# Eight products that nobody reads, and a subtraction one place earlier, in the prologue of a fused RWKV and gated-MLP kernel

## The chip, the cores and the metric

The kernel runs on one core of a Trainium2 chip. The metric is the device time of one execution in microseconds (us); for a kernel it is the median over its runs. The engines are called as in the profile: PE (TensorE, matrix products; PEld is its weight load), DVE (VectorE), ACT (ScalarE), POOL (GpSimd) and SP (SyncE, which here issues every DMA).

## The reference, cut to what matters

For `x` of 4 x 2048 x 512 float32, the layer adds two branches to its input. Both start from the normalised rows:

```python
def _layernorm(x, axis=-1, eps=1e-05):
    m = jnp.mean(x, axis=axis, keepdims=True)
    v = jnp.var(x, axis=axis, keepdims=True)
    return (x - m) / jnp.sqrt(v + eps)

xn = _layernorm(x, axis=-1)
# attention branch: shifted = xn one token later
xk = mu_k * xn + (1.0 - mu_k) * shifted      # the same for xr, xv
k = jnp.einsum('btc,hc->bth', xk, Wk)        # the same for r, v
wkv = wkv_v4(k, v, wkv_w, wkv_u)             # a recurrence over the tokens
attn = jnp.einsum('bth,ch->btc', jax.nn.sigmoid(r) * wkv, Wo)
# MLP branch
hidden = jax.nn.silu(xn @ W1.T) * (xn @ W3.T)
mlp = fwht(hidden) @ W2.T                    # Walsh-Hadamard transform
out = x + attn + mlp
```

The kernel applies the Walsh-Hadamard transform once, to `W2`, in its prologue.

## The kernel before, in words

The 8192 tokens are worked off in 8 pairs of two blocks of 512 tokens. For each pair there are 16 steps with the up weights (`up_step`), then 24 units with the weights of k, v and r of the next pair (`r_unit`) in turn with 20 down products. Every number is split into a rounded high part and a low rest, so each product of a 128 x 128 weight tile takes three matmuls, L953 to L955 in `r_unit`: twelve matmuls for a unit. ACT makes the high part, DVE (inputs, L1403) or POOL (weights, L751, first pair alone) the low part. The weights are split during the first pair and stored; from the second pair on they are only loaded.

Every engine has its own program, in the order in which it is written; semaphores join them. The change lies in the prologue, ahead of pair 0:

- The inputs of the first pair lie in `xt`, channels on partitions. To normalise them, the mean and the reciprocal deviation of each token must stand in every partition. DVE takes the statistics of the rows (`token_stats`, `token_mean_var`, `add_eps`). `make_diagonal(0, 0)` (L1354) puts the 4 x 128 means on diagonals of 128 x 128 tiles, and `spread_tokens(0)` on PE (L977) multiplies them by a matrix of ones, `had[:, 3, :]`; four products fill bank `acc[0]` with the mean of every token. The same is done with the reciprocal deviation, which POOL makes (L745), by `make_diagonal(0, 1)`, into `acc[1]`.
- `centre(0, 0, pair)` (L1368) subtracts `acc[0]` from two of the four channel tiles of the first 512 tokens, `scale(0, 0, pair)` (L1380) multiplies them by `acc[1]`. `centre` waits for the first half of `xt` and for the four products of the means; `scale` for the four products of the deviations.
- Then the inputs of unit n are mixed: ACT `mix_first` (L1035), DVE `mix_item` (L1394), ACT `mix_second` (the high part, L1047), DVE `mix_rest` (the low part, L1403), and PE multiplies. There are three buffers: `mix_second(n)` waits from n = 3 on for unit n - 3 to be done.
- After units 0 to 8 PE makes the first half of the transform of `W2` (`turn_within_tiles`, L988: sixteen products of a constant float32 matrix by a float32 tile of 512 columns), spreads the tokens of the second block (L977 again), and goes on with the units. After unit 14 comes the second half (L967), then the rest and pair 0.
- DVE computes the statistics of the second block, `first_stats(1)` (L1322 and behind), between the mixing for units 4 and 5.

Of the kernel before, what the change touches and what calls it, by code (L numbers as in the profile page):

```python
# [128 lines left out]
def build(nc, x, x_t, w_units, vectors, hadamard, out):  # L129
# [15 lines left out]
    with ctx:  # L145
        def sb(name, shape, dt=f32, stack=ctx):
            return stack.enter_context(nc.sbuf_tensor(name, shape, dt))
# [6 lines left out]
        acc = [ctx.enter_context(nc.psum_tensor(f"acc{i}", [P, C], f32)) for i in range(TT)]  # L154
# [23 lines left out]
        with ExitStack() as early:  # L178
            had = sb("had", [P, 4, P], f32, early)
# [108 lines left out]
        def wait(eng, s, t, k):  # L288

            value = t * per[s.name] + k  # L290
            if not isinstance(value, int) or value > 0:
                eng.wait_ge(s, value)
# [504 lines left out]
        def _(pe):  # L797
# [136 lines left out]
            def r_unit(r, n):  # L934

                g, kt = divmod(n, KT)
                w = r_weights(r, n)
                m_in = mix[n % MIX_AHEAD]
                wait(pe, mix_hi, r, n + 1)
                wait(pe, mix_lo, r, n + 1)  # L940
                for m in range(KT):
                    if kt == 0 and g:
                        wait(pe, kvr_ready, r, KT * (g - 1) + m + 1)
                    elif kt == 0:
                        if m == 0:
                            wait(pe, ha_full, r - 1, FT)
                        elif m == 1:
                            wait(pe, gate_a_sum, r - 1, FT)
                        else:
                            wait(pe, gate_b_sum, r - 1, FT)  # L950
                    col = slice(m * P, (m + 1) * P)
                    bank = r_bank[m]
                    pe.matmul(bank[:, :], w[:, 0, col], m_in[:, 0, :], start=kt == 0, stop=False)  # L953
                    pe.matmul(bank[:, :], w[:, 1, col], m_in[:, 0, :], start=False, stop=False)  # L954
                    last = pe.matmul(bank[:, :], w[:, 0, col], m_in[:, 1, :], start=False, stop=kt == KT - 1)  # L955
                    if m == KT - 1:
                        last.then_inc(r_done, 1)
                    elif kt == KT - 1:
                        last.then_inc(r_bank_done, 1)

            def turn_across_tiles():

                wait(pe, xt_ready, 0, 4)
                for n, j in enumerate(TILES_TURNED):
                    pe.wait_ge(turned_loaded[j * W2_LOADS // FT], 16)
                    pe.wait_ge(w2_copied, FT + n + 1 - TT)
                    pe.matmul(acc[j % TT][:, :], had[:, 1, :], fly[0][:, j, :], start=True, stop=True)\  # L967
                        .then_inc(w2_psum, 1)

            def spread_tokens(h):  # L970

                for a in range(2):
                    if h:
                        pe.wait_ge(w2_copied, FT - 1 + a)
                    for t in range(TT):
                        pe.wait_ge(diagonal_made, 2 * TT * h + TT * a + t + 1)
                        last = pe.matmul(acc[2 * h + a][:, t * P:(t + 1) * P], had[:, 3, :], diagonal[:, a, t, :],  # L977
                                         start=True, stop=True)
                    last.then_inc(spread, 1)

            def turn_within_tiles():

                wait(pe, xt_ready, 0, 2)
                for j in range(FT):
                    pe.wait_ge(w2_loaded[j * W2_LOADS // FT], 16)
                    if j >= TT:
                        pe.wait_ge(w2_copied, j + 1 - TT)
                    pe.matmul(acc[j % TT][:, :], had[:, 0, :], fly[0][:, j, :], start=True, stop=True)\  # L988
                        .then_inc(w2_psum, 1)

            pe.wait_ge(had_loaded, 16)
            spread_tokens(0)
            for n in range(R_UNITS):
                r_unit(0, n)
                if n == PASS_ONE_AFTER:
                    turn_within_tiles()
                    spread_tokens(1)
                if n == PASS_TWO_AFTER:
                    turn_across_tiles()
# [310 lines left out]
        def _(dve):  # L1310
            def wide(a):
                return a.broadcast_to([P, 2, N])
# [29 lines left out]
            def columns(h, pair):  # L1342
                return xt[:, 2 * pair:2 * pair + 2, 1 + h * N:1 + (h + 1) * N]

            def spread_row(h, a):
                return acc[2 * h + a][:, :].rearrange("p (o n) -> p o n", o=1)

            def make_diagonal(h, a):

                if h:  # L1350
                    dve.wait_ge(spread, a + 1)
                    dve.wait_ge(rstd_ready if a else mean_copied, 2)
                for t in range(TT):
                    dve.tensor_scalar(diagonal[:, a, t, :], had[:, 2, :], mean_rstd[:, h, a, t:t + 1], None, ALU.mult)\  # L1354
                        .then_inc(diagonal_made, 1)

            def centre(r, h, pair):

                first = isinstance(r, int) and r == 0
                if pair == 0:  # L1360
                    if first:
                        dve.wait_ge(xt0_loaded[h], 16)
                        dve.wait_ge(spread, 2 * h + 1)
                    else:
                        wait(dve, xt_loaded, r - 1, 64)
                        wait(dve, tok_loaded, r - 1, 16 * (h + 1))
                a = columns(h, pair)
                dve.tensor_tensor(a, a, wide(spread_row(h, 0) if first else tok[:, 0:1, :]), ALU.subtract)\  # L1368
                    .then_inc(centred, 1)

            def scale(r, h, pair):

                first = isinstance(r, int) and r == 0
                wait(dve, centred, r, 2 * h + pair + 1)
                if first:
                    dve.wait_ge(spread, 2 * h + 2)
                elif h == 0 and pair == 1:
                    wait(dve, tok_stored, r - 1, 32)
                a = columns(h, pair)
                dve.tensor_tensor(a, a, wide(spread_row(h, 1) if first else tok[:, 1:2, :]), ALU.mult)\  # L1380
                    .then_inc(xt_ready, 1)
# [336 lines left out]
                .then_inc(const_made, 1)  # L1718
            dve.wait_ge(decay_made, 2)
            dve.wait_ge(pro_step, 8)  # L1720
            dve.wait_ge(rstd_ready, 1)
            make_diagonal(0, 1)
            centre(0, 0, 0)
            scale(0, 0, 0)
            centre(0, 0, 1)
            mix_item(0, 0)
# [71 lines left out]
```

## Time and profile before

| | us |
|---|---|
| median of 3 runs | 2708.76 (2707.26 to 2709.22) |
| the profiled execution | 2706.29 |
| its span, first to last instruction | 2704.5 |
| PE busy | 2658.3 (98%) |
| DVE busy | 2177.0 (80%) |
| ACT busy | 1328.5 (49%) |
| POOL busy | 237.0 (9%) |

Busy times of PE overlap in their ends, since a matmul is started before the one ahead of it has left the array: the start of one matmul to the start of the next is the better measure, and a row with the first and last start of a group gives it. PEclk is the granted clock of PE as a share of 2.4 GHz.

### The profile page before, as it was taken

How to read it: one execution, taken by the hardware profiler on the slowest of the kernel's cores; microseconds unless marked ns; L12 is line 12 of the kernel's file. 1: busy time of each engine (PE TensorE's matmuls, PEld its weight loads, DVE VectorE, ACT ScalarE, POOL GpSimd, SP SyncE). 2: the span in 40 equal slices, each digit the busy share in tenths (PEclk: the TensorE clock that was granted, in tenths of full speed). 3: DMA queues.
4: the chain of work that ended last, by engine and by line, in shares of the span. 5: the costliest groups of instructions: out<-in, count | busy, mean ns of one | idle time of the engine just before them, and what ended most of it. 6: DMA issues, size and time to landing. Idle time of an engine off the chain costs nothing.

```text
span 2704.5 us, 33906 instructions
## 1 busy us (share of the span) xinstructions
PE 2658.3 (98%) x11616; PEld 2178.5 (81%) x11616; DVE 2177.0 (80%) x2938; ACT 1328.5 (49%) x2117; POOL 237.0 (9%) x180
## 2 busy tenths in 40 slices
PE   7999999999999999999999999999999999999998
PEld 5677787888888888888888888888888888888887
DVE  7888888888868888688887888868888788878784
ACT  6765564444554446444464445544455444544442
POOL 3388800000000000000000000000000000000000
PEclk9999999999999999999999999999999999999999
DMA  7787786877868778687787867778687777866677
GB/s 274 293 300 256 280 287 221 278 241 244 286 218 280 241 249 279 231 271 235 254 277 240 279 217 270 259 247 271 216 278 248 261 258 232 273 240 221 230 227 267
DMA packets 244952, 691.51 MB, mean 256 GB/s; under 512 B 31920, under 2 KB 31920, under 8 KB 244272
## 3 DMA queue, kind: packets, MB, share of 16 engines
q1 hardware_dynamic: 244784, 689.34, 75.7%
q8 instruction: 97, 1.59, 0.2%
q14 instruction: 71, 0.58, 0.1%
HBM read 575.94 MB, written 113.30 MB: 255 GB/s over the span
## 4 chain that ended last, share of the span: by engine, by line
PE 89%; DVE 5%; POOL 2%; ACT 1%; issue 1%; DMA 1%; SPq 0%; ACTq 0%; DVEq 0%
PE gamma L871 12%; PE gamma L874 12%; PE gamma L873 12%; PE acc L881 10%; PE acc L883 10%; PE acc L882 10%; PE gamma L953 4%; PE gamma L955 4%; PE gamma L954 4%; PE alpha L871 2%; PE alpha L873 2%; PE alpha L874 2%; PE alpha L955 1%; PE alpha L953 1%; PE alpha L954 1%
## 5 line engine op out<-in xcount | busy, mean ns | idle before, releaser
L1069 ACT ACTIVATE step<-gamma 128x512 f32<-128x512 f32 x512 | 306.3, 598 | 823.1 <-PE gamma L874 807.1
L871 PE MATMUL gamma<-xs_high,wring 128*128 128x512 f32 x1280 | 499.3, 390 | 12.2 <-DVE step L1522 5.4
L873 PE MATMUL gamma<-xs_high,wring 128*128 128x512 f32 x1280 | 498.4, 389 | 0.0
L874 PE MATMUL gamma<-xs_low,wring 128*128 128x512 f32 x1280 | 498.4, 389 | 0.0
L881 PE MATMUL acc<-vring,hid 128*128 128x512 f32 x1232 | 481.0, 390 | 8.2 <-POOL vring L751 4.0
L883 PE MATMUL acc<-vring,hid 128*128 128x512 f32 x1232 | 479.6, 389 | 0.0
L882 PE MATMUL acc<-vring,hid 128*128 128x512 f32 x1232 | 479.6, 389 | 0.0
L871 PEld LDWEIGHTS gamma<-xs_high,wring 128*128 128x128 f32 x1280 | 240.5, 188 | 65.5 <-issue 8.6
L881 PEld LDWEIGHTS acc<-vring,hid 128*128 128x128 f32 x1232 | 231.4, 188 | 62.4 <-issue 9.1
L874 PEld LDWEIGHTS gamma<-xs_low,wring 128*128 128x128 f32 x1280 | 240.5, 188 | 50.2
L873 PEld LDWEIGHTS gamma<-xs_high,wring 128*128 128x128 f32 x1280 | 240.5, 188 | 49.6
L883 PEld LDWEIGHTS acc<-vring,hid 128*128 128x128 f32 x1232 | 231.4, 188 | 48.1
L882 PEld LDWEIGHTS acc<-vring,hid 128*128 128x128 f32 x1232 | 231.5, 188 | 47.4
L1394 DVE SCALAR_TENSOR_TENSOR step<-xt,vec,step 128x512 f32<-128x512 f32 x192 | 144.8, 758 | 141.9 <-ACT step L1035 141.3
L1047 ACT ACTIVATE mix<-step 128x512 fp32r<-128x512 f32 x192 | 120.8, 629 | 239.7 <-PE gamma L955 187.4
L1482 DVE RECIPROCAL z<-z 128x512 f32<-128x512 f32 x64 | 214.1, 3345 | 0.0
L953 PE MATMUL gamma<-mix,wring 128*128 128x512 f32 x522 | 203.6, 390 | 4.6 <-ACT kvr L1062 2.6
L955 PE MATMUL gamma<-mix,wring 128*128 128x512 f32 x522 | 203.1, 389 | 0.0
L954 PE MATMUL gamma<-mix,wring 128*128 128x512 f32 x522 | 203.1, 389 | 0.0
L745 POOL TENSOR_TENSOR mean_rstd<-var_eps,half 128x4 f32<-128x4 f32 x16 | 23.1, 1447 | 1882.7 <-DVE var_eps L1340 1882.7
L1530 DVE TENSOR_TENSOR step<-step,alpha 128x512 f32<-128x512 f32 x128 | 86.4, 675 | 120.9 <-PE alpha L874 101.7
L1403 DVE TENSOR_TENSOR mix<-step,mix 128x512 fp32r<-128x512 f32 x192 | 137.7, 717 | 20.7 <-ACT mix L1047 10.3
(177 smaller groups left out, 4745.3 us busy)
## 6 DMA issues: line engine op xcount, KB each, us to landing
wring<-u_split SPq DMA_DIRECT2D x336, 512.0 KB, 4.2
vring<-d_split SPq DMA_DIRECT2D x288, 512.0 KB, 4.3
wring<-r_split SPq DMA_DIRECT2D x168, 512.0 KB, 4.2
raw<-spilled SPq DMA_DIRECT2D x160, 256.0 KB, 4.2
spilled<-step SPq DMA_DIRECT2D x128, 256.0 KB, 4.3
wlast<-u_split SPq DMA_DIRECT2D x112, 256.0 KB, 3.1
u_split<-wring SPq DMA_DIRECT2D x48, 512.0 KB, 3.9
res<-x SPq DMA_DIRECT2D x16, 1024.0 KB, 8.2
```

Of the source, the lines that this page charges most:

```text
L871: pe.matmul(bank[:, :], w[:, 0, col], high, start=fresh and kt == 0, stop=False, skip_group_check=True)
L873: pe.matmul(bank[:, :], w[:, 1, col], high, start=False, stop=False, skip_group_check=True)
L874: last = pe.matmul(bank[:, :], w[:, 0, col], low, start=False, stop=kt == 1, skip_group_check=True)
L881: pe.matmul(acc[tt][:, :], a[:, 0, col], w[:, 0, :], start=first, stop=False)
L882: pe.matmul(acc[tt][:, :], a[:, 1, col], w[:, 0, :], start=False, stop=False)
L883: return pe.matmul(acc[tt][:, :], a[:, 0, col], w[:, 1, :], start=False, stop=final)
L953: pe.matmul(bank[:, :], w[:, 0, col], m_in[:, 0, :], start=kt == 0, stop=False)
L954: pe.matmul(bank[:, :], w[:, 1, col], m_in[:, 0, :], start=False, stop=False)
L955: last = pe.matmul(bank[:, :], w[:, 0, col], m_in[:, 1, :], start=False, stop=kt == KT - 1)
L1069: act.activation(to, bank[:, :], ACT.Copy).then_inc(u_copied, 1)
L1394: dve.scalar_tensor_tensor(f, xt[:, kt, 1 + h * N:1 + (h + 1) * N], vec[:, q, kt:kt + 1], f, ALU.mult, ALU.add).then_inc(mix_full, 1)
L1482: dve.reciprocal(z[:, 1, :], z[:, 1, :]).then_inc(wkv_step, 1)
```

## The change

Two edits, both ahead of unit 0. PE issues eight products of the constant matrix of ones by the constant tiles `had` (512 float32 columns) between `spread_tokens(0)` and unit 0; they go to `acc[2]` and `acc[3]` in turn, wait for nothing, signal nothing, and what they leave there is overwritten by the next product that starts in these banks. And DVE subtracts the mean from the first two channel tiles, `centre(0, 0, 0)`, ahead of the second diagonal instead of behind it.

```diff
             pe.wait_ge(had_loaded, 16)
             spread_tokens(0)
+            for i in range(8):
+                pe.matmul(acc[2 + i % 2][:, :], had[:, 3, :], had[:, :, :].rearrange("p a q -> p (a q)"),
+                          start=True, stop=True)
             for n in range(R_UNITS):
                 r_unit(0, n)
...
             dve.wait_ge(decay_made, 2)
             dve.wait_ge(pro_step, 8)
+            centre(0, 0, 0)
             dve.wait_ge(rstd_ready, 1)
             make_diagonal(0, 1)
-            centre(0, 0, 0)
             scale(0, 0, 0)
             centre(0, 0, 1)
```

DVE before, from the diagonals of the means to the mixing for the first two units (`tok` holds the diagonals, `acc` the spread values):

```order
L1354 TENSOR_SCALAR tok<-had,mean_rstd 128x128 x4
L1717 TENSOR_SCALAR one_less_mu<-vec 128x12
L1354 TENSOR_SCALAR tok<-had,mean_rstd 128x128 x4
L1368 TENSOR_TENSOR xt<-xt,acc 128x2x512
L1380 TENSOR_TENSOR xt<-xt,acc 128x2x512
L1368 TENSOR_TENSOR xt<-xt,acc 128x2x512
L1394 SCALAR_TENSOR_TENSOR step<-xt,vec,step 128x512 x2
```

DVE in the changed kernel, the same place (its lines stand three further down the file):

```order
L1357 TENSOR_SCALAR tok<-had,mean_rstd 128x128 x4
L1720 TENSOR_SCALAR one_less_mu<-vec 128x12
L1371 TENSOR_TENSOR xt<-xt,acc 128x2x512
L1357 TENSOR_SCALAR tok<-had,mean_rstd 128x128 x4
L1383 TENSOR_TENSOR xt<-xt,acc 128x2x512
L1371 TENSOR_TENSOR xt<-xt,acc 128x2x512
L1397 SCALAR_TENSOR_TENSOR step<-xt,vec,step 128x512 x2
```

The first subtraction has gone ahead of the four diagonals of the deviation; nothing else moved on DVE.

PE at the start of its program, as a difference (`first_r` holds the split weights of units 0 to 3):

```order
 L796 UNCONDITIONAL_BRANCH
 L977 MATMUL acc<-tok,had 128x128 x8
+L994 MATMUL acc<-had 128x512 x8
 L953 MATMUL gamma<-mix,first_r 128x512
 L954 MATMUL gamma<-mix,first_r 128x512
```

The eight products stand between the products that spread the tokens and the first matmul of unit 0.

## Rows read from the trace of the kernel before

**Rows 1.** The page: busy time of PE, and the chain that ended last by engine.

```profile
PE 2658.3 (98%) x11616; PEld 2178.5 (81%) x11616; DVE 2177.0 (80%) x2938; ACT 1328.5 (49%) x2117; POOL 237.0 (9%) x180
...
PE 89%; DVE 5%; POOL 2%; ACT 1%; issue 1%; DMA 1%; SPq 0%; ACTq 0%; DVEq 0%
```

**Rows 2.** Windows (us): busy us (and count) by engine, clock, DMA share, GB/s.

```profile
0.00:130.00 130.00, 111.91 (x429) 80.06 (x430) 102.89 (x143) 89.88 (x149) 39.03 (x33) 0.99 0.76 281
...
340.00:2704.00 2364.00, 2351.68 (x10349) 1940.57 (x10347) 1895.52 (x2611) 1114.47 (x1760) 18.41 (x13) 1.00 0.76 252
```

**Rows 3.** Timeline of DVE: start us, us, what, [idle before <-releaser].

```profile
7.72 0.87 DVE L1354 TENSOR_SCALAR tok<-had,mean_rstd 128x128 f32<-128x128 f32 x4
...
9.21 0.87 DVE L1354 TENSOR_SCALAR tok<-had,mean_rstd 128x128 f32<-128x128 f32 x4 [0.54 <-POOL mean_rstd L745]
10.31 1.22 DVE L1368 TENSOR_TENSOR xt<-xt,acc 128x1024 f32<-128x1024 f32 x1 [0.22 <-PE acc L977]
12.02 1.22 DVE L1380 TENSOR_TENSOR xt<-xt,acc 128x1024 f32<-128x1024 f32 x1 [0.48 <-PE acc L977]
...
24.21 1.80 DVE L1403 TENSOR_TENSOR mix<-step,mix 128x512 fp32r<-128x512 f32 x1
...
26.60 1.79 DVE L1403 TENSOR_TENSOR mix<-step,mix 128x512 fp32r<-128x512 f32 x1
28.31 1.27 DVE L1322 BATCH_NORM_STATS2 stats<-x 128x6 f32<-128x512 f32 x2
...
31.64 0.75 DVE L1394 SCALAR_TENSOR_TENSOR step<-xt,vec,step 128x512 f32<-128x512 f32 x1
32.30 0.69 DVE L1403 TENSOR_TENSOR mix<-step,mix 128x512 fp32r<-128x512 f32 x1
```

**Rows 4.** Timeline of PE: tokens spread, first matmuls of units 0, 1, 5, and L988.

```profile
8.15 3.75 PE L977 MATMUL acc<-tok,had 128*128 128x128 f32 x16 [8.15 <-DVE tok L1354]
...
16.57 0.76 PE L953 MATMUL gamma<-mix,first_r 128*128 128x512 f32 x1 [4.66 <-DVE mix L1403]
...
20.71 0.40 PE L953 MATMUL gamma<-mix,first_r 128*128 128x512 f32 x1
...
33.13 0.47 PE L953 MATMUL gamma<-mix,wring 128*128 128x512 f32 x1 [1.03 <-ACT mix L1047]
...
44.12 4.45 PE L988 MATMUL acc<-fly,had 128*128 128x512 f32 x10
```

**Rows 5.** Matmuls of three lines (L977 twice): ns min/median/max, first and last start.

```profile
L977 PE MATMUL acc<-tok,had x16: 421/421/552, 8.2 to 11.5; 128*128 128x128 f32 x16
...
L977 PE MATMUL acc<-tok,had x16: 275/275/369, 57.9 to 59.6; 128*128 128x128 f32 x16
...
L988 PE MATMUL acc<-fly,had x32: 590/592/592, 44.1 to 57.4; 128*128 128x512 f32 x32
```

**Rows 6.** Windows of PE alone: busy us (and count), clock, DMA share, GB/s.

```profile
12.58:15.99 3.41, 0.00 (x0) 1.00 1.05 386
15.99:19.40 3.41, 2.83 (x7) 0.50 1.05 387
...
234.44:237.86 3.42, 3.42 (x10) 0.50 0.28 104
```

**Rows 7.** Timeline of PE before and behind the second low-clock stretch.

```profile
233.59 0.47 PE L871 MATMUL gamma<-xs_high,wring 128*128 128x512 f32 x1 [3.30 <-DVE step L1522]
...
249.73 0.47 PE L881 MATMUL acc<-vring,hid 128*128 128x512 f32 x1 [1.34 <-POOL vring L751]
```

**Rows 8.** Timeline of ACT: the high parts for units 3 and 4.

```profile
22.27 0.63 ACT L1047 ACTIVATE mix<-step 128x512 fp32r<-128x512 f32 x1 [0.62 <-DVE step L1394]
...
24.33 0.63 ACT L1047 ACTIVATE mix<-step 128x512 fp32r<-128x512 f32 x1 [0.30 <-DVE step L1394]
```

**Rows 9.** Timeline of POOL: two weight splits.

```profile
24.11 1.36 POOL L751 TENSOR_TENSOR wring<-res,wring 128x512 fp32r<-128x512 f32 x1 [0.71 <-ACT wring L1160]
...
26.18 1.67 POOL L751 TENSOR_TENSOR vring<-res,vring 128x512 fp32r<-128x512 f32 x1 [0.71 <-ACT vring L1160]
```

## The prediction, made before the changed kernel ran

> **What bounds the kernel now.** I read the page first: PE is busy 98% of the span and holds 89% of the chain that ended last [rows 1]. By stage it is the same picture with one weak place: from 340 us on PE is busy 2351.7 of 2364 us, in the first 130 us only 111.9 of 130 [rows 2]. So a stall in the prologue has no slack to vanish into later: whatever PE does later there, the steady part behind it starts later. The change touches only the stretch up to 44 us, so the next view is the timeline there, engine by engine. The reader is to see three things.
>
> First, DVE sets the start. The means' diagonals start at 7.72 and PE answers at 8.15, 0.43 later; the deviation's diagonals run from 9.21 to 10.08; the first subtraction starts at 10.31, released by PE's first four products, and the first scaling at 12.02, released by the next four [rows 3, 4]. Unit 0 starts at 16.57, when its inputs are mixed, after PE sat idle for 4.66 us [rows 4].
>
> Second, the clock. PE runs the sixteen matmuls of the spread from 8.2 to 11.5, a pitch of 3.3 / 15 = 0.22 us; the same sixteen take 57.9 to 59.6 later, 1.7 / 15 = 0.11 us [rows 5]. So the first ones ran at 1.2 GHz, though no low clock is recorded for them. Then the records show the high level from 12.58 to 15.99 with PE idle, the low one from 15.99 to 19.40, and the high one again [rows 6]: the fall follows the idle time, the rise comes 2.8 us after PE restarted at 16.57. Unit 0 therefore takes 20.71 - 16.57 = 4.14 us. Four units at the high clock take 44.12 - 33.13 = 10.99, 2.75 each [rows 4], so the low clock costs unit 0 1.39 us.
>
> Third, unit 5, at 33.13, is where PE last waits in this stretch, 1.03 us [rows 4]. What it waits for is DVE: the statistics of the second block from 28.31, then the mixing for unit 6 at 31.64 and the low part for unit 5 at 32.30, which ends at 32.99 [rows 3]. From 33.13 to 44.12 and into the transform PE has no gap. So the change is worth what it moves unit 5.
>
> **The subtraction moved.** It waits for the first four spread products, and these end where they did: the subtraction had waited 0.22 us for PE behind the second diagonals, not for DVE [rows 3]. It cannot start before 10.31. The slot it leaves, 9.21 to 10.08, was filled with the second diagonals beside PE's work; now DVE waits there, and the diagonals start behind the subtraction, at 10.31 + 1.22 = 11.53. From the start of the first diagonals to the start of what waits for their products took 10.31 - 7.72 = 2.59 us, at the low clock (0.43 to PE, 2.16 from there). So the first scaling starts at 11.53 + 2.59 = 14.12 instead of 12.02: +2.1 us. At the high clock eight matmuls with a pitch of 0.11 instead of 0.22 save 0.8 to 0.9: +1.2. No cover hides it, since all mixing waits for it. Nothing is gained in exchange; a gain would need the subtraction earlier, which the 0.22 us excludes.
>
> **The eight products.** The trace shows their like: L988 is a constant float32 matrix by 512 float32 columns; 32 matmuls for sixteen products from 44.1 to 57.4, a pitch of 13.3 / 31 = 0.43 us at the high clock [rows 5]. Eight products are 16 matmuls: 6.9 us at the high clock, 13.7 at the low one. They start behind the spread: its second half starts at 11.53 + 0.43 = 11.96 and takes 8 x 0.213 = 1.7, so 13.7. The 4.66 us of idle that they are put into is shorter than the cheapest of the two. Where the clock rises at time w, they end at 13.7 + 6.9 + (w - 13.7) / 2. In before the high level stood at the latest 12.58 - 8.15 = 4.4 us after PE first started and came 2.8 us after it restarted; 2.8 to 4.4 behind 11.96 is w = 14.8 to 16.4. I take w = 16, the end of the range, because PE also pauses from about 10.2 to 11.96: end at 21.7. The bounds: high throughout, with a spread that ends at about 13.1, gives 20.0; w = 19.4 gives 23.4; never gives 27.4.
>
> Unit 0's inputs are ready at 16.57 + 2.1 = 18.7, so the products, not the inputs, now hold unit 0. It starts at 21.7 at the high clock: +5.1 on its start, but it takes 2.75, not 4.14, +3.7 on its end. Units 0 to 4 back to back are 5 x 2.75 = 13.7, so PE could start unit 5 at 35.4, +2.3; the rest of the +3.7 goes into the 1.03 us before unit 5 and small gaps before it.
>
> DVE comes out alike. The high part of unit 3 waits for unit 0 to be done: 21.7 + 2.75 + 0.2 = 24.65, against 22.27, +2.4; that of unit 4 for unit 1: 27.4, against 24.33, +3.1 [rows 8]. DVE is busy with earlier low parts in between, so the statistics start +2.4 to +2.8 late, and unit 5 with them. The two do not add: one late start of unit 5, the later of PE's +2.3 and DVE's +2.4 to +2.8. I take +2.6.
>
> The DMA queue is no price: the loads of W2, issued behind splits that shift too, are needed at 44.12 + 2.6.
>
> By the Trainium skill's page "TensorE: Matmul & The Clock Gate" (What's actually happening), the throttled clock is the default and activity releases it, which speaks for the products as warm-up; the low stretch behind the idle time agrees. Its whole worth here would be the 1.39 us of unit 0, and the sum without the products' own length would be 1.39 us shorter, not 2.6 longer.
>
> Two low parts, at 24.21 and 26.60, take 1.8 us where that at 32.30 takes 0.69 [rows 3]; POOL's splits started at 24.11 and 26.18, ahead of them [rows 9]. If shifted starts avoid one, DVE is 1.1 us earlier, but PE's 35.4 then holds unit 5: +2.3 stays. The page "SBUF — State Buffer" of the Trainium skill (SBUF: two separate sides) calls the pair of ports that the two engines share an exclusive lock held for the whole instruction; these rows agree.
>
> **Behind 44 us** all is moved by the same amount. One term can differ: a second low stretch, 234.44 to 237.86, after an idle time of 3.30 us [rows 6, 7]. If it falls away, PE gains up to 3.42 / 2 = 1.7 us; but PE then waits 1.34 us for POOL at 249.73, so most of it would only lengthen that wait. I take 0, with -1.7 to +1.7 as bounds.
>
> **Sum.** The profiled execution: 2706.29 + 2.6 = 2708.9. It lies 2.5 under the median, so the forecast for the median is 2708.76 + 2.6 = 2711.4.
>
> **The rivals.**
> - High clock from the start (17%): the high level of 12.58 is granted here too. For it: the record. Then products end at 20.0, unit 5 by PE at +0.6, DVE at +1.2 to +1.5: about 2710.1.
> - Late rise (17%), w = 19.4, since the pause at 10.2 counts against the rise: products end at 23.4, unit 5 at +4.0: 2712.8.
> - The clock never rises before unit 0 (5%): products end at 27.4, unit 5 at +8.0: 2716.8. Against: in before it rose within 2.8 us of dense work.
> - Absorbed (9%): later waits of pair 0, such as 3.30 and 1.34 us [rows 7], turn out to wait for something that did not shift. Against: DMA and all engines hang on PE's transform. 2708.8.
> - The clock pays, the other side (4%): with the high clock from the start (+1.2) and the second low stretch gone (-1.7), the kernel is faster, 2708.3. Place: 234 us; it decides once the shift is under 1.7 us and pair 0 there waits for PE, against which POOL's wait speaks. A version in which unit 0's 1.39 us also counts would need the products done by 16.6, which the pitch of L988 excludes.
>
> **How the numbers follow.** The forecast, with a shift of 2.3 to 2.8, has 48%: 2711.4. A measurement tells 0.2%, 5.4 us, from no change. Only the never-rising clock passes it, so slower by over 0.2% has 5% and 3 more for spread and for two terms at their far ends together: 8%. Faster by as much follows from no case; 2% for what I don't see. Within 0.2%: 90%. The range goes from 2707.6 (the clock pays, and a run 0.7 low) to 2715.2 (late rise, +1.7 of the second stretch and 0.7).
>
> **What would show it.** In the profile of the changed kernel: DVE idle from about 8.7 to 10.3, the subtraction still at 10.31, the scaling at about 14.1 (13.2 would be the high clock); the new matmuls at a pitch of 0.85 and then 0.43, end near 21.7; unit 0 with a pitch of 0.23 and 2.75 us long; unit 5 near 35.7 and the transform near 46.7; the same shift at the end. Wrong would be a scaling at 12.0, products with a pitch of 0.23 or less, or a transform shifted by over 2 us with an end that is not.

## The result, and the profile after

| | before | changed |
|---|---|---|
| median of 22 runs each, in turn | 2707.97 us (2703.52 to 2712.24) | 2711.95 us (2706.88 to 2715.96) |
| ratio, 95% interval | | 1.0013 (1.0008 to 1.0019) |
| profiled execution, its span | 2706.29, 2704.5 | 2706.88, 2705.1 |

The changed kernel is slower by 0.13%, 3.5 us (2.2 to 5.1 by the interval; the two medians themselves stand 4.0 us apart). The profiled execution of it happens to be the quickest of its 22, only 0.6 us above that of before; why is told below. Where the time goes must be read at the start.

DVE of the changed kernel answers to [rows 3]:

```profile
10.31 1.22 DVE L1371 TENSOR_TENSOR xt<-xt,acc 128x1024 f32<-128x1024 f32 x1 [1.66 <-PE acc L977]
11.45 2.46 DVE L1357 TENSOR_SCALAR tok<-had,mean_rstd 128x128 f32<-128x128 f32 x4
15.34 1.22 DVE L1383 TENSOR_TENSOR xt<-xt,acc 128x1024 f32<-128x1024 f32 x1 [1.42 <-PE acc L977]
...
30.89 1.80 DVE L1406 TENSOR_TENSOR mix<-step,mix 128x512 fp32r<-128x512 f32 x1
32.61 1.27 DVE L1325 BATCH_NORM_STATS2 stats<-x 128x6 f32<-128x512 f32 x2
...
36.59 0.69 DVE L1406 TENSOR_TENSOR mix<-step,mix 128x512 fp32r<-128x512 f32 x1
```

The subtraction starts at 10.31 to the hundredth, as before. The four diagonals behind it take 2.46 us, not 0.87, and the first scaling starts at 15.34, 3.3 us late. Three views show why, in this order: the diagonals singly (ns min/median/max, first and last start), POOL's work beside them, and the timeline of PE, which answers to [rows 4]:

```profile
L1357 DVE TENSOR_SCALAR tok<-had,mean_rstd x4: 273/564/1298, 11.4 to 13.6; 128x128 f32<-128x128 f32 x4
```

```profile
10.95 2.49 POOL L751 TENSOR_TENSOR first_r<-raw,first_r 128x512 fp32r<-128x512 f32 x2 [1.90 <-ACT first_r L1163]
```

```profile
8.13 2.05 PE L977 MATMUL acc<-tok,had 128*128 128x128 f32 x8 [8.13 <-DVE tok L1357]
12.36 0.80 PE L977 MATMUL acc<-tok,had 128*128 128x128 f32 x2 [2.18 <-DVE tok L1357]
13.58 1.65 PE L977 MATMUL acc<-tok,had 128*128 128x128 f32 x6 [0.42 <-DVE tok L1357]
15.02 8.34 PE L994 MATMUL acc<-had 128*128 128x512 f32 x16
22.80 0.80 PE L953 MATMUL gamma<-mix,first_r 128*128 128x512 f32 x1
...
25.96 0.39 PE L953 MATMUL gamma<-mix,first_r 128*128 128x512 f32 x1
...
37.42 0.47 PE L953 MATMUL gamma<-mix,wring 128*128 128x512 f32 x1 [0.39 <-ACT mix L1050]
```

POOL splits the first two weight tiles from 10.95 to 13.44, about 1.25 us each. Taken singly, the first diagonal runs from 11.45 to 12.30 and the second from 12.22 to 13.52; the splits end at 12.22 and 13.44. So each of the two diagonals ends 0.08 us behind the end of a split, and the other two, with POOL idle, take 0.27 us each. The same 0.08 stands in the two other profiles with this order and POOL beside it (the changed kernel again, and the move alone). POOL's own row for these splits in the kernel before, which no diagonal met there, since the last one ended at 10.08:

```profile
10.80 2.49 POOL L751 TENSOR_TENSOR first_r<-raw,first_r 128x512 fp32r<-128x512 f32 x2 [1.73 <-ACT first_r L1160]
```

PE gets the first diagonal's work at 12.36 and the second's at 13.58. The products start at 15.02 and the last begins at 22.8; unit 5 starts at 37.42 instead of 33.13, +4.3, and the transform, by the row below, at 48.45 instead of 44.12. The products have their forecast pitch: the row of L994 (ns min/median/max, first and last start), the windows of PE (busy, clock, DMA share, GB/s), which answer to [rows 5, 6], and PE at the transform:

```profile
L994 PE MATMUL acc<-had x16: 592/592/1061, 15.0 to 22.8; 128*128 128x512 f32 x16
```

```profile
15.02:17.65 2.63, 2.63 (x5) 1.00 1.06 389
17.65:22.80 5.15, 5.15 (x14) 1.00 0.79 267
22.80:25.96 3.16, 3.16 (x15) 1.00 0.79 245
140.53:143.94 3.41, 3.31 (x8) 0.50 0.83 266
234.44:237.86 3.42, 0.12 (x2) 1.00 0.89 326
```

```profile
48.45 1.02 PE L988 MATMUL acc<-fly,had 128*128 128x512 f32 x2
```

Up to 17.65 us four of the new matmuls start (five with the last of the spread), behind that one every 0.43 us: the clock was low until about there, though the column says 1.00, since the records start only at 17.65. Unit 0 runs at the high clock: behind the last product, which ends at about 23.2, it takes 2.75 us. ACT's high part for unit 3 waits for it, at 26.21 instead of the 22.27 of [rows 8]:

```profile
26.21 0.63 ACT L1050 ACTIVATE mix<-step 128x512 fp32r<-128x512 f32 x1 [1.27 <-PE gamma L955]
```

By the windows the stretch of low clock at 234 us [rows 6] is missing in this execution, and one at 140 us is there.

### The profile page after: what moved, and what is told of

Same layout as the page of the kernel before. It is cut to its first block, busy times and chain, and to the rows that moved or that the text cites. A ratio compares the mean times of both kernels' runs of the same rounds, so it can differ in the third digit from the quotient of the medians.

```text
span 2705.1 us, 33938 instructions
## 1 busy us (share of the span) xinstructions
PE 2664.4 (98%) x11632; PEld 2181.5 (81%) x11632; DVE 2176.6 (80%) x2938; ACT 1328.1 (49%) x2117; POOL 236.7 (9%) x180
## 4 chain that ended last, share of the span: by engine, by line
PE 89%; DVE 5%; POOL 3%; ACT 1%; issue 1%; DMA 1%; SPq 0%; ACTq 0%; DVEq 0%
PE gamma L871 12%; PE gamma L874 12%; PE gamma L873 12%; PE acc L881 10%; PE acc L883 10%; PE acc L882 10%; PE gamma L953 4%; PE gamma L955 4%; PE gamma L954 4%; PE alpha L871 2%; PE alpha L874 2%; PE alpha L873 2%; PE alpha L953 1%; PE alpha L955 1%; PE alpha L954 1%
## 5 line engine op out<-in xcount | busy, mean ns | idle before, releaser
L882 PEld LDWEIGHTS acc<-vring,hid 128*128 128x128 f32 x1232 | 231.4, 188 | 47.4
L745 POOL TENSOR_TENSOR mean_rstd<-var_eps,half 128x4 f32<-128x4 f32 x16 | 22.6, 1414 | 1880.2 <-DVE var_eps L1343 1880.2
```

The lines of the kernel that those rows point to most:

```text
L882: pe.matmul(acc[tt][:, :], a[:, 1, col], w[:, 0, :], start=False, stop=False)
```

## The experiments

What a profile's matmuls show is given as the start of the transform (44.12 in the kernel before), since the same matmul can be found in each; beside it stands the start of DVE's first scaling. Except in the last column each figure is of one execution. The ratio compares with the kernel before, run in turn with it.

| | transform at | first scaling at | median, ratio (95%) |
|---|---|---|---|
| before, changed | 44.12, 48.45 | 12.02, 15.34 | 1.0013 (1.0008 to 1.0019) |
| the same, second profiles | 44.17, 48.11 | 12.07, 15.11 | |
| move alone | 48.15 | 16.06 | 2710.73, 1.0012 (1.0003 to 1.0022) |
| products alone, and again | 44.00, 44.45 | 11.87, 12.18 | 2707.72, 0.9996 (0.9987 to 1.0005) |
| changed, POOL waits | 46.92 | 14.06 | 2709.32, 1.0008 (0.9999 to 1.0017) |
| move alone, POOL waits | 46.24 | 14.03 | 2709.71, 1.0011 (1.0002 to 1.0020) |
| sixteen products | 51.21 | 11.98 | 2713.41, 1.0020 (1.0010 to 1.0029) |
| statistics split | 43.53 | 12.15 | 2706.50, 0.9999 (0.9990 to 1.0008) |
| three products and split | 43.20 | 12.21 | 2707.10, 0.9999 (0.9990 to 1.0008) |

### The move alone

```diff
 # the changed kernel
             spread_tokens(0)
-            for i in range(8):
-                pe.matmul(acc[2 + i % 2][:, :], ...)
```

> The subtraction moved, without the eight products. Theory A (the move costs more than forecast, because the second diagonals now run beside POOL's first weight splits): the four diagonals take about 2.5 us, the first scaling starts at 15.3 us (12.02 in the kernel before), unit 0 at 16.57 + 3.3 = 19.9, unit 5 and the transform 3.3 us late (36.4 and 47.4), the end +3.3 us. Theory B (the move costs its 2.1 us and the rest of the 4.3 us is the products'): scaling at 14.1, transform at 46.2. Theory C (the move is free without the products): transform at 44.1 to 44.5. PE is idle ahead of unit 0 as before, so its first matmuls are expected at the low clock (pitch 0.43 us) under all.

Its DVE and PE rows:

```profile
8.12 0.87 DVE L1354 TENSOR_SCALAR tok<-had,mean_rstd 128x128 f32<-128x128 f32 x4
10.74 1.22 DVE L1368 TENSOR_TENSOR xt<-xt,acc 128x1024 f32<-128x1024 f32 x1 [1.66 <-PE acc L977]
11.88 2.76 DVE L1354 TENSOR_SCALAR tok<-had,mean_rstd 128x128 f32<-128x128 f32 x4
16.06 1.22 DVE L1380 TENSOR_TENSOR xt<-xt,acc 128x1024 f32<-128x1024 f32 x1 [1.42 <-PE acc L977]
```

```profile
20.60 0.77 PE L953 MATMUL gamma<-mix,first_r 128*128 128x512 f32 x1 [4.65 <-DVE mix L1403]
37.14 0.47 PE L953 MATMUL gamma<-mix,wring 128*128 128x512 f32 x1 [0.93 <-ACT mix L1047]
```

The slow diagonals are the move's, without any product. The transform is 4.03 us late, and the scaling 4.04: what DVE is late arrives one for one. In this execution everything began 0.4 us late (first diagonals 8.12 against 7.72), and the diagonals took 2.76; the rest, 3.6, is what theory A named, a little more. B (2.1) and C (0) are out. The median agrees: +0.12%.

### The products alone, twice

```diff
 # the changed kernel
-            centre(0, 0, 0)
             dve.wait_ge(rstd_ready, 1)
             make_diagonal(0, 1)
+            centre(0, 0, 0)
             scale(0, 0, 0)
```

> The eight products, with DVE's order as in the kernel before. The scaling stays at 12.0. The products start at 11.7 and are 16 matmuls of 0.43 us at the high clock and 0.85 at the low one: with a rise at about 16 us they end at 20.7, unit 0 starts there at the high clock (2.75 us long). Theory A: PE holds unit 5 to at least 20.7 + 13.7 = 34.4, and ACT's high parts, which wait for finished units, hold it to 34.4 to 34.9, so the transform is 1.3 to 1.8 us late (45.4 to 45.9) and the end with it. With no rise before 19.4 us: +3.0. Theory B (the warm clock pays for them): transform at 44.1 or earlier.

> The eight products alone, a second profile. In the first PE had the high clock from 11.4 us on, the products ended by 18.5 and the transform was at 44.0. Theory A (their price follows the time at which the clock rises): with the rise at time w behind 11.7 the transform is at the later of 44.1 and 31.6 + w / 2 + 11.7 - 5.85 - ... that is: 44.0 if w is under about 14, 45.3 at w = 16.5 and up to 46.7 at w = 19.4. Rival (always hidden): 44.0 to 44.2 whatever w.

The rows of L994 and PE's wait ahead of unit 5, in the first of the two:

```profile
L994 PE MATMUL acc<-had x16: 592/592/595, 11.6 to 18.0; 128*128 128x512 f32 x16
```

```profile
32.99 0.47 PE L953 MATMUL gamma<-mix,wring 128*128 128x512 f32 x1 [0.71 <-ACT mix L1050]
```

All sixteen matmuls ran at the high clock (none longer than 595 ns), ended at 18.5, and unit 5 stood at 32.99, before where it was. Theory A's +1.3 to +1.8 rested on a rise of the clock at 16 us, which did not happen: it came by 11.6. With that early rise my own sum, 18.5 + 13.7 = 32.2, is below DVE's 33.0, so nothing is lost. In the second profile the first matmul was slow (1044 ns), the clock's record starts at 12.8, and the transform was at 44.45, 0.33 later than in the kernel before; 0.16 of that is the whole execution being late (scaling 12.18 against 12.02). The formula in the second expectation is garbled. Its 44.0 for so early a rise was missed by 0.45 and the rival's 44.2 by 0.25; the figures for a rise at w = 14 and later were not put to the test, since the rise was early both times. The timing shows no cost (0.9996), and by its interval none above 1.4 us.

### The changed kernel with POOL's first split behind the diagonals

```diff
 # the changed kernel
             inverse_root(0, 0)
+            pool.wait_ge(diagonal_made, 8)
             for n in range(12):
                 lo(("r", n))
```

> The changed kernel, with POOL's first weight split made to wait until all eight diagonals are written, so that the two do not run side by side. Theory A (collision with POOL): the four diagonals take 0.87 us again instead of 2.46, the scaling starts at 14.1 (15.34 in the changed kernel), the products end at about 21.9 to 22.3 instead of 23.2, and the transform is at 47.0 to 47.4 instead of 48.45. Rival (the diagonals are slow behind the subtraction for a reason of DVE's own): they still take 2.4 us and nothing moves.

```profile
10.40 1.22 DVE L1372 TENSOR_TENSOR xt<-xt,acc 128x1024 f32<-128x1024 f32 x1 [1.64 <-PE acc L978]
11.54 0.87 DVE L1358 TENSOR_SCALAR tok<-had,mean_rstd 128x128 f32<-128x128 f32 x4
14.06 1.22 DVE L1384 TENSOR_TENSOR xt<-xt,acc 128x1024 f32<-128x1024 f32 x1 [1.65 <-PE acc L978]
```

```profile
12.49 2.49 POOL L751 TENSOR_TENSOR first_r<-raw,first_r 128x512 fp32r<-128x512 f32 x2 [3.46 <-DVE tok L1358]
```

Same kernel, same products, the diagonals at 0.87 us again and the scaling at 14.06. The collision with POOL is the cause of the 2.46, and DVE's own reason is out. The transform is 1.5 us earlier than in the changed kernel, at 46.92: +2.8, beside the forecast's +2.6, which was made without the collision. The rest of the forecast's sum fits this execution too: the clock's record starts at 15.88 (w = 16 in the prediction), the products run from 13.75 to about 21.7 (13.7 and 21.7), and unit 5 starts at 35.91 (35.7):

```profile
L995 PE MATMUL acc<-had x16: 592/592/1061, 13.7 to 21.2; 128*128 128x512 f32 x16
```

```profile
35.91 0.47 PE L954 MATMUL gamma<-mix,wring 128*128 128x512 f32 x1 [0.39 <-ACT mix L1051]
```

The expectation's own figure for the transform, 47.0 to 47.4, was a little too late. The timing, 1.0008 (0.9999 to 1.0017), can be told neither from the changed kernel's nor from no change, so the 1.5 us is a reading of profiles.

### The move alone with POOL behind the diagonals

```diff
 # the kernel of "the move alone"
             inverse_root(0, 0)
+            pool.wait_ge(diagonal_made, 8)
```

> The subtraction moved, no products, and POOL's first weight split behind the eight diagonals. Theory A (the move costs 2.1 us of order and 1.3 us of collision with POOL; what DVE is late passes on to unit 5 one for one): diagonals 0.87 us, scaling at 14.1, unit 5 and the transform +2.0 to +2.1 us (35.2 and 46.2), end +2.1. Rival (the move passes on less once the collision is gone, since unit 5's wait absorbs it): under +1.0.

Scaling at 14.03, unit 5 at 35.20, transform at 46.24: +2.1, as theory A had it. So the order alone costs 2.1 us, and all of it is passed on. Against the move alone the timing (1.0011 and 1.0012) shows no difference; it is too coarse for 1.3 us.

### Sixteen products

```diff
 # the kernel of "the products alone"
-            for i in range(8):
+            for i in range(16):
```

> Sixteen products instead of eight, with DVE's order as in the kernel before. Theory A (eight were hidden only because unit 5 waits for DVE anyway; a further one costs its length): 32 matmuls of 0.43 us from 11.7 end at 25.4 at the high clock, unit 5 at 25.4 + 13.7 = 39.1, transform at 50.1: +6.0, and the end +6 us; with 2 us of low clock at the start, +7. Rival (such products are cheap for PE whatever their number): transform within 1 us of 44.1.

```profile
L994 PE MATMUL acc<-had x32: 592/592/1061, 11.7 to 25.6; 128*128 128x512 f32 x32
```

```profile
40.22 0.47 PE L953 MATMUL gamma<-mix,wring 128*128 128x512 f32 x1 [0.39 <-ACT mix L1050]
```

The transform is 7.1 us late and the median 6.3 above its own before: eight products more, 16 x 0.43 = 6.9 us, at their full length. They were never cheap; the first eight fit behind DVE.

### The statistics in two halves

```diff
 # the kernel before
-                if n == 1:
-                    first_stats(1)
+                if n in (1, 4):
+                    first_stats(1, [n // 4])   # one half of the rows each time
```

> The kernel before with one edit: the statistics of the second block in two halves, one where they were and one three units later. Theory A (unit 5 waits for DVE, for the statistics): the wait of 1.03 us ahead of unit 5 goes, unit 5 at 31.9 instead of 33.1, the transform at 42.9 to 43.4, 0.7 to 1.2 us early, the end 0.7 to 1.2 us less (below what timing can tell). Rival (unit 5 waits for ACT, as the row names it): the wait stays, 44.1.

```profile
28.43 1.27 DVE L1322 BATCH_NORM_STATS2 stats<-x 128x6 f32<-128x512 f32 x2
...
29.90 1.08 DVE L1394 SCALAR_TENSOR_TENSOR step<-xt,vec,step 128x512 f32<-128x512 f32 x1
30.91 0.68 DVE L1403 TENSOR_TENSOR mix<-step,mix 128x512 fp32r<-128x512 f32 x1
```

The low part for unit 5 is there at 31.6, 1.4 us earlier than in [rows 3], and PE has no wait left between unit 0 and the transform. So it was DVE that held unit 5, not ACT, which the row of PE names. The gain is 0.6 us (43.53), just under the forecast's 0.7 to 1.2: unit 0 kept the low clock longer in this execution, its first matmul at 16.70 and unit 1's at 21.60, 4.9 us, and PE became the bound.

### Three products and the split

The same split, and ahead of unit 0 three of the products where the split alone has none.

> Three products, which fit into PE's idle time, DVE's order as before, statistics in two halves. If PE keeps the high clock for unit 0, it takes 2.75 us instead of 4.14. Theory A (unit 5 is held by DVE up to the split, and behind it by PE and DVE nearly alike): transform at 42.5 to 43.2, at most 0.5 us earlier than with the split alone. Rival (the warm clock is worth its 1.39 us in full): 1.4 us earlier than with the split alone, 41.5 to 42.0.

```profile
16.76 0.47 PE L953 MATMUL gamma<-mix,first_r 128*128 128x512 f32 x1 [1.71 <-DVE mix L1406]
26.35 0.47 PE L953 MATMUL gamma<-mix,first_r 128*128 128x512 f32 x1 [1.15 <-DVE mix L1406]
```

Here PE waits only 1.71 us ahead of unit 0 and keeps the high clock: unit 1 started at 19.60, so unit 0 took 2.84 us. Unit 1 is 2.0 us earlier than with the split alone, but 1.15 us turns into a wait for DVE at unit 3, and the transform moves only from 43.53 to 43.20. Theory A holds, and neither kernel can be told from the one before by its time.

### The unchanged kernels once more

> The kernel before, unchanged, for a second profile of it. Up to 200 us its matmuls should stand within 0.3 us of the first profile, or the shifts read between two profiles are worth less than that. The open point is the low-clock stretch: if it belongs to the program's gap at 230 us it comes back at 234; if it depends on when the clock's decisions fall, it stands elsewhere or is missing, and the time behind it differs by up to 1.7 us.

> The changed kernel, unchanged, for a second profile. Theory A (order and collision set the shift): diagonals 2.5 us, scaling at 15.3 to 15.8, transform at 48.2 to 48.7 whatever the clock does at the start. Open: whether a low-clock stretch follows the idle time near 234 us. If it does, the end stands at about +4 us against the first profile of the kernel before; the first profile of the changed kernel had none there and came out 1.6 us shorter behind it.

Windows of PE in the second profile of the kernel before:

```profile
137.28:140.69 3.41, 3.41 (x10) 0.50 0.63 219
232.85:239.68 6.83, 6.05 (x14) 0.50 0.59 203
```

The second profile of the kernel before agrees with the first to 0.05 us at unit 0, unit 5 and the transform. Between them, at unit 1, it was 0.87 us late, since the clock rose later, and that was gone at unit 5: DVE holds it. The second of the changed kernel has the diagonals at 2.30 us, the scaling at 15.11 and the transform at 48.11: each just below what A named, and far from the kernel before.

The low stretches are where the profiles differ. The kernel before had one at 234.44 [rows 6] and in its second profile one at 137.28 and a double one at 232.85; the first profile of the changed kernel had one at 140.53 and none at 234, the second one at 153.7 and one at 239.0. Take the same matmul of PE in two profiles, the 801st (221.75 us in the kernel before, the added products not counted) and the 851st (238.24): the first profile of the changed kernel is 4.19 us late at the one and 2.59 at the other; the second is 4.42 late at both. So the missing stretch gave back 1.6 us in the execution shown. The move alone and the three products, which had none near 234 us either, gained 1.6 us between the same two matmuls. Later places gave back more (1.1 us between the matmuls 4000 and 7000, 0.7 in the last 600); their cause was not followed up.

The places are not arbitrary. The twelve profiles have 29 low stretches ahead of the last 3 us, counting that of [rows 6] at 15.99, and each of them begins between 0.8 us ahead of the end of a wait of PE of 2.0 us or more (the longest 4.66) and 1.4 us behind it. Between 135 and 154 us, near 235 and near 433 PE waits so in every profile, and a low stretch stands there in ten, nine and six of the twelve. What decides whether one comes was not tested.

## Why the prediction was right, and where it was wrong

**The time.** 2711.95 was measured, 2711.4 forecast, inside the range, and within 0.2% as forecast with 90%. But the shift that makes the time was mis-sized: +2.6 forecast, +4.3 and +4.0 in the two profiles at the transform, +3.5 by timing. That the median came so close is in part luck: the forecast was added to a median of three runs, 2708.76, and the 22 runs have 2707.97. On that base the same sum gives 2710.6, 1.4 us short.

**The subtraction cannot start earlier.** Right, to 0.01 us.

**The diagonals moved: the step that failed.** "So the first scaling starts at 11.53 + 2.59 = 14.12": 15.34 was measured. The term took over a duration of 0.87 us, which the row shows for a time with POOL idle, and moved it to a time at which POOL splits weights. The two POOL splits from 10.80 to 13.3 of the kernel before were in the timeline, and so was the collision, which the prediction read from two low parts and then weighed only as a possible gain. With POOL out of the way 14.06 and 14.03 were measured. The order costs 2.0 us, the collision 1.3. The Trainium skill's page "SBUF — State Buffer" (Who interferes with whom) states that the pair of ports that DVE and POOL share is an exclusive lock; the prediction used this for the low parts and not for the diagonals. These traces agree: each of two diagonals ended 0.08 us behind a POOL split. But not every POOL instruction beside them does this: the first four diagonals ran beside POOL's small L745 (128 x 4, 7.93 to 9.05 in the changed kernel) and took 0.87 us.

**The products.** Their pitch (0.43 and 0.85 us) and that they hold unit 0 were right: they ended at about 23.2, and the formula 15.02 + 6.9 + (17.65 - 15.02) / 2 gives 23.2. Of the 1.5 us beyond the forecast's 21.7 the later start (15.02 for 13.7) makes 0.7 and the later rise of the clock (17.65 for 16) 0.8. With POOL waiting both were as forecast, and so was the 21.7; that the late rise follows from the late start is likely from these two profiles, not shown. In the sum that PE's +2.3 and DVE's +2.4 to +2.8 do not add was right too: with these 1.5 us the one late start of unit 5 becomes +4.1, and +4.29 was measured. What the prediction did not say is how little the products cost by themselves: nothing that can be told, and 0.7 to 1.0 us on top of the move (46.92 - 46.24, the two kernels with POOL waiting; 4.33 - 3.32, the shifts of the transform and of the scaling in the changed kernel). The move, not the products, is most of the change's price.

**The clock of unit 0.** It came: 2.75 us from the end of the products, as forecast. The forecast set its 1.39 us against the products' length on both paths to unit 5, and in the changed kernel it is not measured apart from them. By itself it was seen in the three products with the split: unit 0 took 2.1 us less than with the split alone (2.84 for 4.90), and the transform came 0.33 earlier, since the next waits are for DVE.

**Behind 44 us.** The shift is carried: 4.33 at the transform, 4.2 at 220 us. The term taken as 0 with bounds of 1.7 was one execution's -1.6; that POOL's wait would absorb it was wrong for that execution (PE waited 1.35 us there, 1.34 before). For the median it is spread between runs.

**The rivals.** "High clock from the start" is what the first profile of the products alone showed, without the move, and there the products cost nothing; in the changed kernel the clock rose at 17.65, between the forecast's 16 and the late rise's 19.4. Absorbed and never-rising did not occur, nor "the clock pays".

## What to carry to other kernels

A duration belongs to what runs beside it: when an instruction is moved, look at what the engine that shares its ports does at the new time, before its old duration goes into the sum. Filler work for PE's clock is free only while something else holds the next wait, and its gain is lost by the same wait; find that wait first. The two profiles of the kernel before agree to 0.05 us at the transform and those of the changed kernel to 0.34; at the end the latter differ by 2.1 us. So a shift of 0.1% is read at the first matmul behind the change, and not at the end of one profile.

## What the runs showed of the hardware

- Four tensor-by-scalar instructions of 128 x 128 float32 on DVE took 0.87 us alone and 2.30 to 2.76 beside two POOL tensor-tensor instructions; the longest single one 1.30 us against 0.28, each slow one ending 0.08 us behind a POOL instruction. A subtraction on DVE with one operand in PSUM took its 1.22 us with POOL's splits beside it as well.
- PE's clock at the start of an execution is low in the durations while the clock column still says 1.00: it says so until its first record. Those lay between 11.4 and 24.3 us.
- The granted clock fell for stretches of 3.4 us, twice 6.8, each time at the end of a wait of PE of 2.0 us or more; the same wait brought one in some executions of a program and none in others. Of 22 runs of the changed kernel the 7 with a mean clock of 0.999 took 2710.0 us on the mean, the 8 with 0.997 took 2713.0.
